# The bias of q, k and v: added once to the weights instead of once per block

## The reference

```python
x = x + L0_attn(layernorm(x))            # fast weights, one sequence after the other
x = x + L0_ffn(layernorm(x))

# L0_ffn, for one sequence
h = attn_norm_w * (x * rsqrt(mean(x * x) + 1e-5))
qkv = h @ qkv_w + qkv_b                  # 16 heads of q, 4 of k, 4 of v, 64 wide: 1536 columns
q, k = rope(q), rope(k)
y = softmax(q k^T / 8, window 128, sink) v
x = x + y @ proj_w + proj_b
# then rmsnorm, gate with top 4 of 32 experts, silu(g) * u, down, weighted sum
```

## Time and profile before

| | us |
|---|---|
| median of 3 runs (lowest, highest) | 1021.84 (1020.54, 1021.86) |
| the profiled execution | 1020.91 |
| its span, first to last instruction | 1019.2 |
| PE busy in the span | 867.9 (85%) |
| DVE busy | 711.4 (70%) |
| ACT busy | 597.6 (59%) |
| POOL busy | 505.0 (50%) |
| PE, 96 bias products of 512 columns (L357, side_q and a score bank) | 35.8 + 1.3 |
| PE, 192 passes of qkv (L552) | 95.9 + 3.1 |

### The profile page before, as it was taken

The page is one execution under the profiler, slowest core; times in us unless marked ns, Lnnn a source line. Parts: engine busy times, 40 slices in busy tenths (PEclk is TensorE's granted clock), DMA queues, the critical chain, the costliest instruction groups (busy, mean ns, idle before and its releaser), DMA issues. The chain is left out here.

```text
span 1019.2 us, 21500 instructions
## 1 busy us (share of the span) xinstructions
PE 867.9 (85%) x6737; PEld 668.7 (66%) x6737; DVE 711.4 (70%) x2456; ACT 597.6 (59%) x1987; POOL 505.0 (50%) x643
## 2 busy tenths in 40 slices
PE   1888999999999999999999999999837988788500
PEld 0455777777777777777777777777616877677400
DVE  2647888989889898898988988888642443333118
ACT  0216786877868768687676877877713644444300
POOL 2223324555455544555445554574361777777750
PEclk7799999999999999999999999999957998899755
DMA  6879999999800000000000000000013444432139
GB/s 159 264 255 374 375 375 375 367 368 369 268 12 14 19 13 18 13 13 21 10 19 16 10 20 10 19 21 21 16 42 90 133 133 131 123 99 74 52 118 332
DMA packets 98369, 131.51 MB, mean 129 GB/s; under 512 B 15025, under 2 KB 54866, under 8 KB 98258
## 3 DMA queue, kind: packets, MB, share of 16 engines
q1 hardware_dynamic: 84690, 108.36, 32.3%
q0 software_dynamic: 9216, 19.68, 5.6%
q10 hardware_dynamic: 4352, 2.10, 0.7%
HBM read 30.34 MB, written 99.75 MB: 128 GB/s over the span
## 5 line engine op out<-in xcount | busy, mean ns | idle before, releaser
L1312 POOL TENSOR_TENSOR l_t_cos<-l_t_cos,l_t_sin 128x512 f32<-128x512 f32 (+1 forms) x96 | 115.0, 1198 | 249.6 <-DVE l_t_sin L905 249.5
L1145 ACT ACTIVATE l_prob<-l_score,l_nm 128x128 f32<-128x128 f32 (+1 forms) x512 | 211.8, 435 | 19.2 <-DVE l_nm L764 18.9
L1518 POOL DMA_INDIRECT expert_out<-e_yo,e_dest x160 | 153.2, 958 | 68.8 <-issue 36.6
L1155 ACT COPY l_probT<-l_turned 128x512 f32<-128x512 f32 x192 | 111.4, 593 | 67.4 <-PE l_turned L393 65.0
L94 POOL DMA_INDIRECT expert_rows<-h,slot x128 | 128.8, 1006 | 40.4 <-issue 34.4
L753 DVE TENSOR_REDUCE l_mx<-l_score 128x2 f32<-128x512 f32 (+1 forms) x192 | 123.4, 684 | 26.6 <-PE l_score L379 25.5
L393 PEld LDWEIGHTS l_turned<-ident_sb,l_prob 128*128 128x128 f32 x768 | 88.0, 141 | 47.9 <-issue 41.8
L1145 ACT ACTIVATION_READ_ACCUMULATOR l_prob<-l_score,l_nm 128x1 f32 x512 | 112.7, 220 | 0.0
L393 PE MATMUL l_turned<-ident_sb,l_prob 128*128 128x128 f32 x768 | 110.3, 276 | 1.3 <-DVE l_prob L738 0.6
L379 PE MATMUL l_score<-l_kT,l_qT 64*128 64x128 f32 (+1 forms) x1024 | 109.8, 343 | 0.0
L408 PE MATMUL l_turned<-l_probT,l_vv 128*64 128x128 f32 x1536 | 105.0, 279 | 1.3 <-ACT l_probT L1155 1.3
(11 more groups left out here) (232 smaller groups left out, 1779.0 us busy)
## 6 DMA issues: line engine op xcount, KB each, us to landing
expert_rows<-zeros SPq DMA_DIRECT2D x32, 2240.0 KB, 22.5
e_xt<-expert_rows SPq DMA_DIRECT2D x160, 70.0 KB
e_rows<-expert_out SPq DMA_DIRECT2D x16, 512.0 KB, 5.9
wup_sb<-in_wup SPq DMA_DIRECT2D x1, 4096.0 KB, 15.2
expert_out<-e_yo,e_dest POOLq DMA_INDIRECT x160
expert_rows<-zeros SPq DMA_DIRECT2D x32, 70.0 KB, 2.5
expert_rows<-zeros SPq DMA_DIRECT2D x4, 560.0 KB, 12.4
expert_rows<-h,slot POOLq DMA_INDIRECT x128, 2.4
```

The source lines that it names most:

```text
L1145: ins = A_.activation(prob[:, b, h, cols], score[(2 * u + h) % 3][:, cols], ACT.Exp, bias=nm[:, b, h, j:j + 1], scale=0.125, accum_out=sum ...
L1155: A_.copy(probT[:, h, :], turned[h][:]).then_inc(s["probT"], 1)
L1312: g.tensor_tensor(t_cos[:, c % 2, 0:w], t_cos[:, c % 2, 0:w], t_sin[:, c % 2, 0:w], ALU.add).then_inc(s["added"], 1)
L1518: g_.indirect_dma_start(m["ys"], bass.IndirectOffsetOnAxis(ap=dest[:, g % FOUND, j:j + 1], axis=0), yo[:, g % YO, j, :], None).then_inc(se ...
```

## The change

The bias goes into the weights. With w the norm's weights, W the weights, b the bias, and S the column sums of diag(w) W over the 128 features, the new weights are W' = diag(w) W + (b - S)/128. Their columns sum to b. If a normalised row r sums to zero, then (r + 1) W' = r diag(w) W + b: the first product loses the added constant because r sums to zero, the second is the column sum. So hT becomes the transposed row plus 1, and the product with the bias is left out of every chunk.

W' is made in iteration n = 1: DVE scales wqkv by -w (L738's operation on 128x1536), PE makes three times the product of ones with the scaled weights plus that of ones with bias3, into the three score banks, which are free then, and DVE joins the two with three instructions. The first chunk of n = 2 waits for the last of them; three waits of PE there (loads, constants, bias) and one of ACT (loads) go or move.

```diff
@@ qkv (PE)
                 if n == 2 and c == 0:
-                    pe.wait_ge(m["attn_loaded"], ATTN_LOADS * 16)
-                    pe.wait_ge(s["constants"], 1)
-                    pe.wait_ge(s["bias_in"], 3 * 16)
+                    pe.wait_ge(s["folded"], 4)
                 dst = chunk_bank(n, c)
                 after(pe, s["qk_out"], N * CHUNKS + c - (1 if n == 2 else 0))
-                bias(dst[:], part * 512, (part + 1) * 512)
                 mm(dst[:], hT[:, t * P:(t + 1) * P], m["wqkv"][:, part * 512:(part + 1) * 512],
-                   start=False, stop=True).then_inc(s["qkv_ps"], 1)
+                   start=True, stop=True).then_inc(s["qkv_ps"], 1)
@@ idle (PE)
                 if 0 <= n < 3:
                     keep_clock(1, turned[0])
+                if n == 1 and u == 5:
+                    pe.wait_ge(s["folded"], 1)
+                    pe.wait_ge(s["bias_in"], 3 * 16)
+                    for k in range(3):
+                        cols = slice(k * 512, (k + 1) * 512)
+                        mm(score[k][:], m["ones"][:], m["wqkv"][:, cols], start=True, stop=False)
+                        mm(score[k][:], m["ones_bf"][:], m["bias3"][:, cols], start=False, stop=True) \
+                            .then_inc(s["fold_ps"], 1)
@@ first_stats (DVE)
+                if n == 1 and u == 3:
+                    v.wait_ge(m["attn_loaded"], ATTN_LOADS * 16)
+                    V.tensor_scalar(m["wqkv"][:], m["wqkv"][:], m["norms"][:, 0:1], -1.0, ALU.mult, ALU.mult) \
+                        .then_inc(s["folded"], 1)
+                if n == 1 and 8 <= u < 11:
+                    cols = slice((u - 8) * 512, (u - 7) * 512)
+                    v.wait_ge(s["fold_ps"], u - 7)
+                    V.scalar_tensor_tensor(out=m["wqkv"][:, cols], in0=score[u - 8][:], scalar=1.0 / P,
+                                           in1=m["wqkv"][:, cols], op0=ALU.mult, op1=ALU.subtract).then_inc(s["folded"], 1)
@@ hT_out (ACT)
-                if n == 1:
-                    act.wait_ge(m["attn_loaded"], ATTN_LOADS * 16)
                 after(act, s["qkv_ps"], O * CHUNKS)
                 act.wait_ge(s["hn_ps"], O + 1)
-                A_.activation(hT[:], side_f[:, 0:TOK], ACT.Copy, scale=m["norms"][:, 0:1]).then_inc(s["hT"], 1)
+                A_.activation(hT[:], side_f[:, 0:TOK], ACT.Copy, bias=1.0).then_inc(s["hT"], 1)
```

More of the change, by code:

```diff
@@ L287, in layers @@
         names = (
-            "filled cleared part constants bias_in ready stat0 rs0 xn xT_ps xT z_ps zT a_ps aT az_ps a_tok z expo gelu tanh slope apdf sloped "
+            "folded fold_ps filled cleared part constants bias_in ready stat0 rs0 xn xT_ps xT z_ps zT a_ps aT az_ps a_tok z expo gelu tanh slope apdf sloped "
             "rT_ps rT hr_ps h r dh_ps da g_ps w out_ps x1 "
```

## The result

The changed kernel takes 1008.30 us (median of four runs, 1007.86 to 1008.52); the kernel before took 1021.79 beside it. The ratio is 0.987, with a 95% interval of 0.9853 to 0.9887. The profiled execution took 1007.86 us with a span of 1006.1.

What follows compares the result with a forecast made beforehand. The loop was taken as PE-bound, with DVE and POOL setting the distance from chunk 2 to the next x_turn. Savings of 11.6 us less startup costs of 1.0 and 3.0 gave -7.6: 1013.8 us as median, range 1004.5 to 1019.5.

Steps and rivals of the forecast that it cites:

- I therefore book 0.65 us for each of the 11 iterations: Loop, n = 5 to 15: dropping the bias products saves 0.65 us an iteration, 7.15 us in all.
- The early chunks' 0.65: Chunks 0 to 2, ahead of DVE's wait: x_turn to rope of chunk 2 becomes 0.65 us shorter.
- PE gains 0.65 us there and waits it out at x_turn: Chunks 3 to 5: DVE and POOL set the distance, so PE's 0.65 us brings nothing.
- rival A: Loop: x_norm slips past the sends and all PE time comes back, 21.0 us less startup's 4.0: 1003.9 us; chance 0.17.
- B: Loop: DVE and POOL hold the whole iteration, startup's 4.0 us stays: 1023.7 us, slower; chance 0.10.
- The scaling: Startup, DVE at n = 1 ahead of x_norm: scaling wqkv costs 1.0 us, not covered.
- The six products: Startup, PE at n = 1: they take 3.24 us, 0.24 covered, so 3.0 us cost.
- hT_out: Copy after x_turn: adding a constant instead of scaling saves 0 to 0.1 us an iteration, off the path; booked 0.
- The three sums: Startup, DVE: at most 0.82 us each, hidden in idle time; without the cover up to 2.5 us in all.
- Rival C: Startup, n = 1: delayed x_norm is caught by POOL's power, losing up to 4.5 us: 1017.8 us; chance 0.08.
- Rival D: Startup and n = 2: PE work falls at 1.2 GHz, losing up to 3.2 us (1016.5), or 1 us won; chance 0.09.
- the period: Loop, one x_turn to the next: 41.6 us if the forecast is right, against 42.24 before.

Runs made afterwards that it cites:

- early_again: Changed kernel with the bias product put back, overwritten, ahead of the qkv products of chunks 0 to 2 alone: 1018.55 us.
- late_again: Changed kernel with the bias product put back, overwritten, ahead of the qkv products of chunks 3 to 5 alone: 1013.52 us.
- middle_again: Changed kernel with the bias product put back, overwritten, at chunks 3 and 4 alone: 1011.78 us.
- last_again: Changed kernel with the bias product put back, overwritten, at chunk 5 alone: 1011.13 us.
- the nudges: Changed kernel with two or four tiny 128x1 additions on DVE ahead of x_norm from n = 5 on: 1010.06 us with two, 1014.94 with four.
- sends_first: Changed kernel with POOL's last two sends of an iteration moved ahead of the norms: 1006.54 us.
- sends_first_before: Kernel before, without the change, with POOL's last two sends of an iteration moved ahead of the norms: 1019.48 us.
- fold_in_idle: Changed kernel with the scaling moved behind x_norm of n = 1 and the product pairs into PE's waits, k's sums to n = 2: 1005.45 us.
- fold_in_idle_sends: fold_in_idle with POOL's last two sends also moved ahead of the norms, as in sends_first: 1001.32 us.

## Why the prediction was right in direction and short in size

**The wrong step.** "I therefore book 0.65 us for each of the 11 iterations": the measured term is 1.02. The early chunks' 0.65 was right (0.64 by early_again). The late chunks' "PE gains 0.65 us there and waits it out at x_turn" was wrong in two places, which late_again measures at 0.39 together. First, DVE's work "almost without a pause" up to the statistics did hold a wait for PE that I did not list, ahead of the maxima: 0.14 us (33.14 and 33.15 against 33.00 in late_again and middle_again). Second, the hold of POOL on x_norm, which I took as fixed, has a step: x_norm starting 0.23 us earlier behind the statistics gets its first instruction ahead of the spread, and x_turn comes 0.24 us earlier. Against rival A I had asked whether x_norm can pass the send; it need not: wherever it had started no more than 0.44 us behind the send's start, its first instruction got in behind the send. last_again and middle_again show the step by their sum (0.19, against 0.39), the nudges by what takes the place. That the time lies in the range all the same is due to its width: it was drawn most of the way to A, and this step was not foreseen.

**Rival A, B.** The loop lies between the forecast (41.6) and A (40.9). A's condition, x_norm past the sends, did not come about, and where an edit brought it about (sends_first against sends_first_before) the change was worth 1.05 us, not 1.3. B, everything held, is ruled out by early_again.

**The startup.** The scaling took 0.99 us for 1.0 and stood ahead of x_norm. The six products took 51.91 - 48.69 = 3.22 us for 3.24; x_turn of n = 2 came 2.35 us later and not 3.0, because PE was at its higher level earlier (granted 0.91 between 45 and 48 us, before 0.74; 0.39 us less from x_turn to the fillers) and because hT_out is now shorter (0.15 us less from norm_turn to x_turn):

```profile
L1219 ACT ACTIVATE l_hT<-l_side_f x16: 384/390/402, 62.5 to 655.9; 128x256 f32<-128x256 f32 x16
```

(480 ns in the earlier trace rows), which I had put off the path; in the startup x_turn of n = 2 waits for it. The three sums took 0.66 to 0.68 us in DVE's idle time, as said.

**Rival C.** Its condition, that the power starts first, did not come about. x_norm's second instruction started at 41.28, the power ran 4.63 us from 41.35, and x_norm took 0.60: not held. The POOL instruction ahead of the power took 0.98 us beside the scaling, 0.30 in the kernel before and in fold_in_idle, where x_norm runs beside it:

```profile
40.29 0.98 POOL L1418 TENSOR_SCALAR l_rstd<-l_mv 128x26 f32<-128x26 f32 x1 [15.34 <-DVE l_mv L1102]
```

So it was held, as the prediction's "against" had it, to 0.16 us behind the end of the scaling. The Trainium skill, SBUF — State Buffer, "Who interferes with whom", says that of DVE and GpSimd, where they contend, the one which issues first has their shared ports for its whole instruction. For the spread the trace agrees (x_norm's second instruction ends only 0.09 us behind it), and for the scaling; beside x_norm POOL's 0.30 us show no hold. Whether the power would have held an x_norm behind it no run shows.

**Rival D.** The products stood at full clock. The low stretch stayed, and moved with the first qkv of n = 2; PE had waited 2.13 us for hn just ahead of it. Granted clock in the column before the last two:

```profile
60.00:63.00 3.00, 0.47 (x3) 0.27 (x4) 1.71 (x5) 0.38 (x1) 1.10 (x3) 0.94 0.58 155
63.00:66.00 3.00, 3.00 (x6) 1.45 (x7) 0.56 (x3) 0.37 (x1) 0.00 (x0) 0.50 0.88 299
```

**The signs.** Right: no bias product in side_q, DVE's wait ahead of chunk 2, the startup's two delays in place. Wrong: the period, and the longer wait of x_turn for x_norm; x_norm moved with PE, and the two meet as before.

## What to carry to other kernels

Before a stretch is booked as set by another engine, list that engine's waits through the whole stretch, the short ones too: each wait for the faster engine gives back part of the gain. Where a short instruction is held by another engine's long ones, its delay goes in steps, so a change of 0.1 us ahead of it can be worth 0.2 or nothing; parts put back singly and together show it, because they don't add up. A one-off price in the startup (3.6 us here) is often a matter of place: the same work in the waits of the same iteration cost almost nothing.

## What the hardware showed unasked

Between POOL's second send and its spread at most one waiting instruction of DVE got through, whatever its size: a 128x1 addition, 0.15 us where nothing holds it, lasted 0.76 us there and cost x_norm its place. An x_norm that started 0.52 us behind the send's start did not get through.

With PE's 2.13 us wait for hn filled, the stretch behind it stood at the higher clock in both kernels with that edit; in the other eleven the granted clock fell to 0.50 there. In fold_in_idle, granted 1.00:

```profile
60.00:63.00 3.00, 3.00 (x12) 1.56 (x11) 1.84 (x6) 0.93 (x3) 0.73 (x1) 1.00 0.58 155
```

In fold_in_idle_sends it is 1.00 there, too. That is 2.4 GHz where the changed kernel has 0.50 (1.2 GHz) in the three microseconds of its first qkv. From x_turn of n = 2 to n = 3 took 23.17 us in both, in the changed kernel 24.66 and in the one before 25.41. In fold_in_idle the lower clock came later, between 83.1 and 86.5 us, and cost 1.7 us there, so that its profile shows no gain from this; PE had waited 0.45 and 0.74 us ahead of it, as it did in fold_in_idle_sends, where the clock stayed at 1.00. There the 1.5 us are a part of the gain beside the moved work. What decides where the clock falls is not shown.
